# Attention in a four-stage kernel: how the reciprocals of the softmax sums reach the partitions of the output

## The reference

```
xn     = layernorm(x_b)                    # 256 rows
q      = xn @ Wq[:, head] ; k, v = xn @ Wkv  (one k and one v for all 16 heads, 64 wide)
s      = q @ [null_k, k].T / 8 + bias      # causal, masked, with one null key ahead
p      = exp(s - max(s))
o      = (p @ [null_v, v]) / sum(p)        # the division the change is about
out_b  = layernorm(sum over heads of o @ Wo[head]) + x_b
```

## Time and profile before

| | |
|---|---|
| median of 3 runs | 890.14 us (889.52 to 890.62) |
| the profiled execution | 891.04 us, of which its span, first to last instruction, 889.3 us |
| PE busy | 785.1 us, 88% of the span |
| VectorE busy | 461.3 us, 52% |
| ScalarE busy | 377.1 us, 42% |
| GpSimd busy | 456.1 us, 51% |
| transfers | 89.41 MB, mean 101 GB/s |
| mean granted TensorE clock | 0.953 of full speed |

### The profile page before, as it was taken

How to read it: one execution, slowest core, us unless ns; L and a number is a source line. 1 busy time by engine, 2 the same in 40 slices (tenths; PEclk the granted TensorE clock), 3 DMA queues, 4 the chain that set the end, 5 groups by cost and what they waited for, 6 DMA issues and landing times.

```text
span 889.3 us, 16732 instructions
## 1 busy us (share of the span) xinstructions
PE 785.1 (88%) x4252; PEld 543.2 (61%) x4253; DVE 461.3 (52%) x1561; ACT 377.1 (42%) x1174; POOL 456.1 (51%) x522
## 2 busy tenths in 40 slices
PE   7868988937999999879999999999999997898891
PEld 3446755824666676647776776767777445675551
DVE  0873434675222222246657566666756387464446
ACT  3323432303333333146656666666666542243330
POOL 1377776006626542254756566475654126777750
PEclk9999999757999999979999999999999999899996
DMA  7863333724544120194010101011000002333346
GB/s 273 320 238 107 102 104 108 222 93 151 175 150 140 60 65 30 60 365 192 1 31 8 37 0 36 0 36 36 0 12 2 24 0 79 107 101 100 104 137 214
DMA packets 45098, 89.41 MB, mean 101 GB/s; under 512 B 7728, under 2 KB 34864, under 8 KB 43504
## 3 DMA queue, kind: packets, MB, share of 16 engines
q1 hardware_dynamic: 30736, 43.80, 14.4%
q0 software_dynamic: 12000, 32.78, 11.9%
q10 hardware_dynamic: 2304, 12.14, 3.5%
HBM read 66.02 MB, written 22.68 MB: 100 GB/s over the span
## 4 chain that ended last, share of the span: by engine, by line
PE 57%; POOL 12%; DVE 11%; DMA 8%; issue 8%; SPq 2%; ACT 2%; DVEq 0%; POOLq 0%; ACTq 0%
PE psH L663 10%; POOL work L958 5%; PE psY L1026 5%; PE psY L680 5%; PE psM L1079 5%; PE psH L1045 5%; PE psM L680 4%; PE psL L1068 4%; PE psHT L1055 4%; POOL d_pairs L966 3%; PE psHT L672 2%; DVE work L890 2%; PE psH L488 2%; PE psY L1031 2%; POOL a_pairs L966 2%
## 5 line engine op out<-in xcount | busy, mean ns | idle before, releaser
L1400 POOL TENSOR_TENSOR work<-work,region_ac 128x386 f32<-128x386 f32 x128 | 119.6, 945 | 91.5 <-ACT work L1152 45.9
L663 PE MATMUL psH<-region_bd,work 128*128 x344 | 126.2, 491 | 0.3 <-ACT work L724 0.3
L1167 ACT ACTIVATE work<-work 128x129 f32<-128x129 f32 (+1 forms) x256 | 114.1, 448 | 11.0 <-DVE work L1262 11.0
L1262 DVE CUSTOM_DVE_ANT_0 work<-psH,work 128x129 f32<-128x129 f32 (+1 forms) x256 | 79.5, 347 | 3.5 <-PE psH L1045 3.5
L771 DVE TENSOR_TENSOR work<-psH,region_bd 128x256 f32<-128x256 f32 (+1 forms) x86 | 46.8, 544 | 64.4 <-PE psH L663 58.1
L966 POOL DMA_INDIRECT b_pairs<-work,home x39 | 37.7, 967 | 74.9 <-DVE work L790 68.1
L663 PEld LDWEIGHTS psH<-region_bd,work 128*128 128x128 f32 x344 | 61.0, 197 | 22.9 <-issue 19.9
L672 PE MATMUL psHT<-ident,work 128*128 128x128 f32 x242 | 49.8, 285 | 24.7 <-DVE work L778 13.9
L672 PEld LDWEIGHTS psHT<-ident,work 128*128 128x128 f32 x242 | 31.7, 141 | 64.6 <-DVE work L778 23.1
L958 POOL DMA_INDIRECT work<-y_scratch,inv x39 | 37.6, 965 | 63.7 <-DVE inv L897 52.1
L1026 PE MATMUL psY<-work,region_ac 128*128 128x256 f32 x256 | 66.8, 384 | 0.5 <-ACT work L1161 0.5
(11 more groups left out here) (225 smaller groups left out, 1612.3 us busy)
## 6 DMA issues: line engine op xcount, KB each, us to landing
region_bd<-in_b_w ACTq DMA_DIRECT2D x2, 4096.0 KB, 21.0
work<-a_pairs SPq DMA_DIRECT2D x16, 256.0 KB, 3.8
work<-b_pairs SPq DMA_DIRECT2D x16, 256.0 KB, 2.9
region_bd<-in_d_w SPq DMA_DIRECT2D x1, 4096.0 KB, 14.7
region_bd<-in_d_b SPq DMA_DIRECT2D x2, 2048.0 KB, 25.5
work<-d_pairs SPq DMA_DIRECT2D x16, 256.0 KB, 3.8
acc<-in_x SPq DMA_DIRECT2D x4, 512.0 KB, 4.6
region_ac<-in_a_gu SPq DMA_DIRECT2D x1, 2048.0 KB, 11.7
```

What stands on the lines that cost most here:

```text
L663: last = pe.matmul(psH[:, h, 0:f.hw], xT[:, h, k, :], f.w_in(k, e), start=(k == 0), stop=(k == KD - 1))
L1167: nc.scalar.activation(c_p[:, o, a:z], c_sc[:, o, a:z], ACT.Exp, scale=-1.0, bias=c_min[:, o, i:i + 1], accum_out=c_sum[:, j % 2, o, i:i + ...
L1400: pool.tensor_tensor(c_bm[:, 2 * (j % 2) + o, :], c_mp, c_bias[:, 2 * j + o, :], ALU.subtract).then_inc(C.bm_ready, 1)
```

## The change

The turning leaves TensorE. `dve_over`, the two transposes of each pair and the second half of `act_queries` go. In their place SP, for each of the 64 pairs, waits for the reciprocals (c_rec2, 128 partitions by four numbers in region_bd), stores them transposed in a DRAM scratch of four rows of 128 numbers, waits for the store to land, and issues two loads, each of which reads one head's 256 reciprocals and repeats them on 64 partitions of c_recB. `dve_o` waits for those (rec_landed) and multiplies by c_recB. The scaling of v goes, since the reciprocals no longer carry the factor.

The order changes too. On VectorE `dve_sums(p)` comes first in the step, and `dve_o(p-1)` moves behind the first head's scores, where `dve_over` stood; a `memset` of one column stands at the end of `dve_scores_wait`. On ScalarE `act_queries(p+2)` moves behind the second head's exponentials. On SP the loop is written out: `sp_spread_rec(p)` for each pair, `sp_pairs(b+2)` after the pair j = 4 of batch b, `sp_store_z(b-1)` after j = 7. `sp_load_d` still stands ahead of all of them.

```diff
         def pe_queries(pe, k, j, odd, b):
...
             wait(pe, C.qr_ready, k)
-            if b is not None:
-                for c in range(KD):
-                    last = pe.matmul(psY[:, 0:SEQ], c_wq[:, c, j * P:(j + 1) * P], c_xnT[:, odd, c, :],
-                                     start=(c == 0), stop=(c == KD - 1))
-            if live(k, -2, 1 << 30):
-                wait(pe, C.rec_ready, k - 1)
-                for i in range(QT):
-                    last = pe.transpose(psY[:, SEQ + i * P:SEQ + (i + 1) * P], c_over[:, i, :, :].rearrange("p o n -> p (o n)"),
-                                        ident[:, :])
+            for c in range(KD):
+                last = pe.matmul(psY[:, 0:SEQ], c_wq[:, c, j * P:(j + 1) * P], c_xnT[:, odd, c, :],
+                                 start=(c == 0), stop=(c == KD - 1))
             last.then_inc(C.qr_mm, 1)
...
             act.wait_ge(C.qr_mm, k + 1)
             wait(act, C.s_mm, k - 1)
-            wait(act, C.o_ready, k - 3)
-            a, z = 0 if new else SEQ, 2 * SEQ if live(k, -2, 1 << 30) else SEQ
-            nc.scalar.mul(c_qr[:, j % 2, a:z], psY[:, a:z], -(float(DH) ** -0.5)).then_inc(C.qr_ready, 1)
+            nc.scalar.mul(c_qr[:, j % 2, :], psY[:, 0:SEQ], -(float(DH) ** -0.5)).then_inc(C.qr_ready, 1)
...
-                act_queries(act, p + 2, j, not (last and j + 2 >= NPAIR))
                 if more:
                     act_exp(act, p + 1, j + 1, 1)
+                if not (last and j + 2 >= NPAIR):
+                    act_queries(act, p + 2, j)
...
         def dve_sums(dve, p, j):
+            wait(dve, C.o_ready, p - 1)
             dve.wait_ge(C.p_ready, 4 * p + 4)
-            nc.vector.reciprocal(c_rec, c_sum[:, j % 2, :, :]).then_inc(C.rec_done, 1)
-
-        def dve_over(dve, p):
-
-            dve.wait_ge(C.rec_done, p + 1)
-            wait(dve, C.qr_mm, p + 2)
-            nc.vector.tensor_copy(c_over, c_rec.rearrange("p o i -> p i o").unsqueeze(3).to_broadcast([P, QT, 2, DH])
-                                  ).then_inc(C.rec_ready, 1)
+            nc.vector.reciprocal(c_rec2[:, j % 2, :], c_sum[:, j % 2, :, :].rearrange("p o i -> p (o i)")).then_inc(C.rec_done, 1)
...
             dve.wait_ge(C.pv_mm, p + 1)
-            dve.wait_ge(C.qr_ready, p + 3)
+            dve.wait_ge(C.rec_landed[j % 2], 32 * half + 32)
             wait(dve, C.wo_mm, p - 1)
-            nc.vector.tensor_tensor(c_oT[:, j % 2, :], psL[:, 0:SEQ], c_qr[:, j % 2, SEQ:2 * SEQ], ALU.mult).then_inc(C.o_ready, 1)
+            nc.vector.tensor_tensor(c_oT[:, j % 2, :], psL[:, 0:SEQ], c_recB[:, j % 2, :], ALU.mult).then_inc(C.o_ready, 1)
...
+        def sp_spread_rec(sp, p):
+
+
+            r = p % 2
+            wait(sp, C.o_ready, p - 1)
+            sp.wait_ge(C.rec_done, p + 1)
+            sp.dma_start(rec_dram[r].rearrange("j t -> t j"), c_rec2[:, r, :], allow_slow_non_contiguous=True).then_inc(C.rec_stored, 16)
+            sp.wait_ge(C.rec_stored, 16 * p + 16)
+            for o in range(2):
+                row = rec_dram[r, QT * o:QT * o + QT, :].rearrange("(a i) t -> a (i t)", a=1)
+                sp.dma_start(c_recB[DH * o:DH * o + DH, r, :], row.to_broadcast([DH, SEQ])).then_inc(C.rec_landed[r], 16)
+
         def sp_attention(sp):
             wait_dmas(sp, B.slots_stored)
             sp_pairs(sp, 0)
             sp_pairs(sp, 1)
             sp_load_d(sp)
-            with sp.Fori(2, BATCH) as b:
-                sp_pairs(sp, b)
-                sp_store_z(sp, b - 2)
-            sp_store_z(sp, BATCH - 2)
+            for p in range(NPAIR * BATCH):
+                b, j = divmod(p, NPAIR)
+                sp_spread_rec(sp, p)
+                if j == 4 and b + 2 < BATCH:
+                    sp_pairs(sp, b + 2)
+                if j == 7 and b > 0:
+                    sp_store_z(sp, b - 1)
             sp_store_z(sp, BATCH - 1)
```

More of the change, by code:

```diff
@@ L1115, in pe_batch @@
                 over = (j + 2) // NPAIR
-                pe_queries(pe, p + 2, (j + 2) % NPAIR, (odd + over) % 2, None if last and over else b + over)
+                if not (last and over):
+                    pe_queries(pe, p + 2, (j + 2) % NPAIR, (odd + over) % 2, b + over)
                 if before:
@@ L1257, in dve_scores_wait @@
             wait(dve, C.p_ready, 4 * p)
+            nc.vector.memset(c_tick, 0.0)
         def dve_scores(dve, p, j, o):
```

47 lines of the change are left out of this document (22 added, 25 removed).

## The result

The changed kernel takes **1298.7 us** (median of 4 runs, 1297.7 to 1300.4) against 890.4 us for the kernel before in the same measurement (889.5 to 892.0). The ratio is 1.4596, with a 95% interval of 1.4574 to 1.4619. The prediction was 921.5 us with a range up to 955. The direction was right. The size was not: the loss is 408 us where 31 were forecast.

The account below looks back on a forecast made before the run. TensorE was taken to bound the kernel before, 4.42 us a pair, and the circle the changed one. 891.0 +18.6 beginning, +5 circle, +5 hiccups, +2.6 end gave 922.2, less 0.9: 921.5 us; range 896 to 955.

Parts of the forecast that it names:

- X: Time for the reciprocals' store to DRAM to land, in SP's queue; taken as 2.6 us.
- near rows: Profile rows bounding the store's landing: a 128 KB store of whole rows, 1.7 us, and nv's 128 single numbers, 2.1.
- Rival 1: SP's serial store and loads set the attention loop's pace once X passes 3.6; about 980 us at X = 4.5; chance 0.24.
- the sum: Whole kernel: 891.0 us plus beginning, circle, hiccups and end, +31, gives 922.2; less 0.9, 921.5.
- hiccups: Late transfers not hidden after `dve_rows`, `sp_pairs` and `sp_store_z`: 0.7 us a batch, +5 us in all.
- the tail: Last pair, where nothing overlaps: reciprocal to `dve_o` 5.4 us instead of 2.77, +2.6 us.
- the wait that I had as hidden: Store and loads of a plain pair, 5.4 us against 6.75 available before `dve_o`: hidden by 1.3 us.
- The circle: Closed chain from scores to scores through ScalarE's later copy of the queries: 4.75 us a pair against 4.42, +5 us.
- The beginning: Attention loop's start: first reciprocals queue behind stage D's weights, 14.8 us stall plus 3.8 for TensorE's slow clock, +18.6 us.
- Rival 3: Loop's beginning is free if small transfers get past the big load: about 903 us; chance 0.10.
- Rival 2: Attention loop runs at TensorE's pace, 4.20 us a pair, the circle being shorter: about 891.5 us; chance 0.08.

Follow-up runs that it names:

- half_store: Changed kernel storing only one head's 256 reciprocals, which both heads' loads read; ratio 1.4106 to the kernel before.
- spread_64B: Changed kernel with each of the 512 4-byte pieces stored in 64 bytes of its own, loads reading another row; ratio 1.0369 to the kernel before.
- spread_16B: Changed kernel with 16 bytes between the starts of the 512 4-byte pieces, loads reading other data; ratio 1.0704 to the kernel before.
- spread_8B: Changed kernel with 8 bytes between the starts of the 512 4-byte pieces, loads reading other data; ratio 1.1575 to the kernel before.
- flat_again: Repeat of flat_store (changed kernel, reciprocals stored unturned as 128 runs of 16 B) where the kernel before takes 890.0 us; 919.9 us, ratio 1.0357.
- both_again: flat_store with queries copied ahead of the second exponentials and stage D's weights issued by ScalarE's queue after the pairs' loads; 895.1 us, ratio 1.0058.
- flat_store: Changed kernel storing the reciprocals unturned, as 128 runs of 16 B instead of 512 of 4 B; 987.2 us, ratio 1.0339 to the kernel before.

## Why the prediction was wrong

**The step that failed is the size of X**, the landing of the store: "I take 2.6, between the near rows". It measured 9.2. Both near rows, the store of whole rows of 128 KB at 1.7 and the 128 single numbers at 2.1, turned out to be of another kind. z_scratch is stored in long pieces and nv is only read from DRAM; here sixteen pieces are written into each 64 bytes. My upper bounds counted issues, 3.5 for four loads one behind the other, and 8.4 wholly in series. The last came close only by chance, since it goes by the count, and half_store with half the count still takes 9.0. Even so, I gave it no weight in the range. A bound that I had worked out and could not exclude by a row belonged in it.

**Rival 1 is what happened**, with the mechanism as written. Its period, 0.1 + X + 0.1 + 0.94, is 10.3 at X = 9.2; SP's rows gave 10.4 for a plain pair and 10.83 in the mean. Put into the sum: 922 + 62 x (10.83 - 4.75) = 1299, and 1298.7 were measured. That it fits to a microsecond is luck: what the hiccups and `pe_kv` add is in the 922 and again in the 10.83 (5 and some 8 x 1.2 us), and of the tail, 13.3 us longer than before, the 922 holds only 2.6. Its threshold, X above 3.6, is less sharp than I had it. In spread_64B, spread_16B and spread_8B (X = 2.3, 3.4 and 5.0) the six middle batches take 241.1, 267.2 and 334.4 us. So 3.4 already costs 26 us: `dve_o` waits for its transfer in 18 pairs there instead of 5, so the wait that I had as hidden comes before SP sets the pace. At 5.0 a pair takes 6.97 in the mean, against 6.14 by the formula. Its chance of 0.24 rested on the two near rows; the price of 57 us was for X = 4.5, half of what X was.

**The circle held.** Predicted 4.75 us a pair, bound by ScalarE's copy behind the second exponentials; in flat_again 4.76 over two pairs, and the wait named in 58. The wait ahead of the scores is 0.39 to 0.61, and 0.55 was forecast. In the changed kernel itself it is covered by the store. **Circle and hiccups** together were 5 + 5; six batches measured +8.5, where 4 + 6 x 0.7 = 8.2 of the forecast fall into them.

**The beginning held**, in the kernel where the store is cheap: `dve_o(0)` forecast at 413.6, measured at 413.86.

```profile
413.86 0.42 DVE L1279 TENSOR_TENSOR work<-psL,work 128x256 f32<-128x256 f32 x1 [15.52 <-DMA work<-rec_scratch]
```

The stretch lost 17.4 us against 18.6. The clock too: these windows of flat_again show TensorE granted 0.50 (1.2 GHz) from 413 to 418, after the pause, and 1.00 (2.4 GHz) again from 420:

```profile
413.00:416.00 3.00, 1.66 (x4) 1.18 (x4) 1.44 (x6) 0.66 (x3) 0.61 (x1) 0.50 0.13 35
416.00:418.00 2.00, 2.00 (x11) 0.95 (x12) 0.18 (x1) 0.59 (x3) 0.25 (x1) 0.50 0.13 27
...
420.00:424.00 4.00, 3.94 (x30) 2.73 (x29) 2.51 (x13) 2.38 (x10) 1.88 (x2) 1.00 0.14 39
```

In the changed kernel the stall came 5.8 us later, by the store's longer landing. Rival 3, a free beginning, is excluded.

**The tail** was forecast at +2.6 and measured +2.7 in flat_again, where the last `dve_o` came 6.0 us after its reciprocal (5.4 forecast). Part of that is luck: its store landed after 1.4 us instead of 2.6, and its loads, issued from 719.51 on, kept `dve_o` until 723.89, 4.4 us where 0.47 + 2.0 were taken. The median load lands after 2.7 us in this run. The stretch also holds the last batch's pairs.

**Rival 2**, TensorE's pace, is false for this change. It became true when the old order came back: 4.19 a pair against the 4.20 worked out. Of the 17 us that it put on six batches, both_again gained 9.1.

**Slips in the arithmetic.** 922.2 less 0.9 is 921.3 and not 921.5, and rival 1 at X = 4.2 gives 960 and not 955. Neither changes the reading.

The Trainium skill (DMA: Bandwidth & Descriptors, Rules for kernel authors) was cited for one descriptor per element. The count alone is not the cause, since 512 elements spread out took 1.9 us. The Trainium skill (the same page, Specifications) says that below 512 B a transfer engine does read-modify-write. The runs agree in so far as pieces that share a stretch hinder each other; that the mechanism is such a read and write of the stretch, one after the other, is argued from the slope of some 0.4 to 0.5 us a piece and not shown. Alone it would not do as a rule either: the pieces of 4 B in 512 B of their own are as small, and cheap, and so are the 16 B pieces of flat_store.

## What to carry to other kernels

A small transfer is not priced by its bytes or its pieces: ask how many separate pieces of 4 B fall into the same short stretch of DRAM (64 bytes here). If a store scatters single numbers, either turn elsewhere and write runs of 16 B, which were cheap here, or give each number 64 bytes of its own. Where an engine or queue handles one round trip per step in series, work out the latency at which it overtakes the present period (3.6 us by the sum here, and 3.4 already cost 26 us) and look for a row that bounds it from above; if none does, the worst bound belongs in the range. And a new small transfer at the start of a loop must be placed in time against the bulk loads that run then, in the same queue and in the others.

## What was not expected of the hardware

- A store of 512 pieces of 4 B that fill 2 KB of DRAM lands after 9.2 us (median), one of 256 that fill 1 KB after 9.0, and one of 512 with 64 or 512 bytes of their own each after 2.3 and 1.9. 128 pieces of 16 B that fill the 2 KB take 1.5.
- During such a store little moves. The one issued at 426.74 landed at 435.94. All packets of SP's queue in between, those of the pair's loads before it among them (two of 64 KB, most of the 58 GB/s below), lie before 430; from 430 to 436 the trace has a single packet, of instructions, and none of the store, although its landing is up to 6 us off. The windows of the changed kernel show it in the last two columns (DMA share and GB/s):

```profile
428.00:430.00 2.00, 0.00 (x0) 0.00 (x0) 0.29 (x1) 0.00 (x0) 0.00 (x0) 1.00 0.41 58
430.00:432.00 2.00, 1.81 (x8) 1.17 (x10) 1.82 (x8) 0.81 (x4) 0.77 (x1) 0.84 0.09 4
432.00:434.00 2.00, 2.00 (x14) 1.18 (x10) 0.18 (x1) 0.45 (x3) 0.10 (x1) 0.50 0.00 0
```

- The same windows show the granted clock (the number before the last two) at 1.00 in a window in which TensorE did nothing, and at 0.50, 1.2 GHz, four microseconds later, when it was busy again. Its mean over the loop is the 0.77 above. What the low clock costs beside SP's pace was not measured apart.
